# Two score products for the second attention: by query for the maxima, turned for the exponentials

## What is computed

```python
q = (query @ w_q.T).reshape(B, T_q, 16, 32)
k = (kv_source @ w_k.T).reshape(B, T_kv, 16, 32)
v = (kv_source @ w_v.T).reshape(B, T_kv, 16, 32)
attn = softmax(einsum('bqhd,bkhd->bhqk', q, k) * 32 ** -0.5, axis=-1)
out = einsum('bhqk,bkhd->bqhd', attn, v).reshape(B, T_q, 512)
return out @ w_o.T
```

## Time and profile before

| | us |
|---|---|
| timed runs, median of 3 | 1249.32 (1249.26 to 1250.52) |
| profiled execution, span | 1257.6 |
| of it, attention1 by itself, t=4 to t=29 | 276.1 to 558.2 |
| PE busy over the span | 1189.3 (95%) |
| DVE, ACT, POOL busy | 950.4 (76%), 708.7 (56%), 589.7 (47%) |

### The profile page before, as it was taken

How to read it: one execution, slowest core, us unless ns; L and a number is a source line. 1 busy time by engine, 2 the same in 40 slices (tenths; PEclk the granted TensorE clock), 3 DMA queues, 4 the chain that set the end, 5 groups by cost and what they waited for, 6 DMA issues and landing times.

```text
span 1257.6 us, 29419 instructions
## 1 busy us (share of the span) xinstructions
PE 1189.3 (95%) x10692; PEld 822.8 (65%) x10692; DVE 950.4 (76%) x2006; ACT 708.7 (56%) x1988; POOL 589.7 (47%) x685
## 2 busy tenths in 40 slices
PE   6888998799999999999999999999999998799996
PEld 3555665588888888786444445777777776466663
DVE  5889898899999999896677777777777775445460
ACT  4377788799899999896344322222222231365552
POOL 0047668737666667733200000445544345466744
PEclk9999999999999999999999999999999999899999
DMA  9522033134445454643870141221314320799987
GB/s 346 210 60 76 1 32 46 43 111 142 165 135 169 159 172 148 181 157 119 153 196 1 41 127 34 68 44 60 69 34 108 96 68 2 220 254 242 256 139 96
DMA packets 157567, 150.28 MB, mean 119 GB/s; under 512 B 78544, under 2 KB 111472, under 8 KB 157424
## 3 DMA queue, kind: packets, MB, share of 16 engines
q1 hardware_dynamic: 139584, 125.94, 35.5%
q0 software_dynamic: 13248, 21.15, 8.9%
q10 hardware_dynamic: 4592, 1.32, 0.6%
HBM read 84.93 MB, written 57.19 MB: 113 GB/s over the span
## 4 chain that ended last, share of the span: by engine, by line
PE 59%; DMA 17%; issue 8%; DVE 8%; POOL 5%; ACT 3%; ACTq 0%; SPq 0%; POOLq 0%; DVEq 0%
PE bank L121 28%; DMA lists<-att_land 14%; PE bank L1503 6%; PE bank L2125 5%; PE bank L955 4%; POOL lists L1629 4%; PE bank L1435 4%; PE bank L1456 3%; PE bank L1450 2%; PE bank L1421 2%; DMA q_rows<-att_land 1%; PE bank L1024 1%; ACT att_land L1353 1%; PE bank L872 1%; PE bank L891 1%
## 5 line engine op out<-in xcount | busy, mean ns | idle before, releaser
L1629 POOL DMA_INDIRECT lists<-att_land x128 | 134.4, 1050 | 310.7 <-DVE att_land L1770 166.8
L1353 ACT ACTIVATE att_land<-bank,att_land 128x120 f32<-128x120 f32 x512 | 178.3, 375 | 11.3 <-DVE att_land L1221 11.2
L2125 PE MATMUL bank<-att_land 128*128 128x512 f16 x768 | 177.3, 381 | 0.6 <-DVE program_logits L1304 0.6
L1952 ACT ACTIVATE att_land<-program_x 128x512 f32<-128x512 f32 x40 | 25.2, 631 | 195.2 <-DVE program_x L2094 165.1
L2125 PEld LDWEIGHTS bank<-att_land 128*128 128x128 f16 x768 | 75.4, 98 | 82.9 <-issue 2.0
L121 PE MATMUL bank<-program_xs,program_wgu 128*128 128x512 f16 x576 | 128.7, 379 | 0.6 <-DVE att_land L1729 0.6
L1353 ACT ACTIVATION_READ_ACCUMULATOR att_land<-bank,att_land 128x1 f32 x512 | 112.8, 221 | 0.0
L121 PE MATMUL bank<-att_land 128*128 128x128 f16 (+1 forms) x1560 | 101.0, 221 | 0.5 <-DVE att_land L1278 0.5
L121 PEld LDWEIGHTS bank<-program_xs,program_wgu 128*128 128x128 f16 x576 | 56.2, 98 | 67.5 <-DVE att_land L1729 1.1
L1221 DVE TENSOR_REDUCE att_land<-bank 128x4 f32<-128x480 f32 x128 | 82.4, 644 | 20.5 <-PE bank L1421 20.1
L1503 PE MATMUL bank<-att_land 128*128 128x512 f16 x384 | 93.4, 379 | 0.0
(11 more groups left out here) (305 smaller groups left out, 2817.2 us busy)
## 6 DMA issues: line engine op xcount, KB each, us to landing
att_land<-q_rows SPq DMA_DIRECT2D x96, 128.0 KB, 2.6
xn_rows<-att_land SPq DMA_DIRECT2D x37, 256.0 KB, 3.7
out_rows<-att_land SPq DMA_DIRECT2D x37, 256.0 KB, 6.4
q_rows<-att_land SPq DMA_DIRECT2D x32, 256.0 KB, 2.9
xt_tiles<-att_land SPq DMA_DIRECT2D x32, 256.0 KB, 2.1
x_rows<-program_x SPq DMA_DIRECT2D x8, 1024.0 KB, 4.8
att_land<-x_rows SPq DMA_DIRECT2D x8, 1024.0 KB, 5.6
program_xs<-xt_tiles SPq DMA_DIRECT2D x28, 256.0 KB
```

The lines of the kernel that those rows point to most:

```text
L1353: last = act.activation(prob[:, c, h, :], ps_s[c % 2][:, h, :], ACT.Exp, bias=nmax[:, u % 2, c, h:h + 1], accum_out=rsum[:, u % 2, n:n + 1])
L1629: pool.indirect_dma_start(out=io["lists"], out_offset=bass.IndirectOffsetOnAxis(ap=index[:, t, k:k + 1], axis=0), in_=load[:, t, k, :], in ...
L2125: last = pe.matmul(ps_y[i][:, :], hid[:, c % 2, a, i * P:(i + 1) * P], wd[:, q, c, :], start=c == 0 and n == 0, stop=c == NC - 1 and n == 2)
```

## The change

`scores` stays, but its result only gives maxima. VectorE splits the negated maxima, divided by 64, into a high and a low f16 part and turns them in blocks of 32x32 (`maxima_turned`); SyncE copies them with four DMAs into partitions 96 and 97 of the packed queries. The keys have the constant 64 in these two rows. `scores_turned` multiplies keys (stationary, 98 rows, 120 columns) by queries (128 columns), so that scores less their maxima come out with the context rows on the partitions; ScalarE takes the exponential twice from PSUM (`exponentials`), once as float32 and once as f16. The transposes and the per-head exponentials with sums go. Residues of groups 0 to 2 are made by GpSimd, of group 3 by VectorE, both from SBUF. The values get a 33rd column of ones, which gives the row sums; head 0 has its own place in another bank (`first_output`). Both norms are applied by ScalarE in one operation (`normalise`), after a tiny one on GpSimd. The weight conversion's three operations go into three steps. There are three packed query buffers, the third in space of `program_xs`; so the second batch of tokens in `shared` waits for all outputs. The orders of all five streams within a step change; JOIN and TAIL don't. Some semaphores of `front` are used again.

```diff
+def key_constants(pool, g, n):
+    two = struct.unpack("<f", struct.pack("<ee", MS, MS))[0]
+    return pool.memset(g.keys[:, n].rearrange("p r n -> p (r n)").bitcast(f32), two)
...
-    spread(sp, g.queries[:, u % 2], io["q_rows"][u], (0, 0, 1), done[u % 2])
+    spread(sp, g.queries[u % 3], io["q_rows"][u], (0, 0, 1), done[u % 3])
...
+        if u < self.first:
+            return
+        pool.wait_ge(self.root, u + 1)
+        pool.tensor_scalar(self.shift[:, d], self.mv[:, d, 0:1], self.rstd[:, d], -1.0, ALU.mult,
+                           ALU.mult).then_inc(self.shifted, 1)
+    def normalise(self, act, g, u):
+        act.wait_ge(self.shifted, u + 1 - self.first)
+        act.activation(self.xn[:, u % 2], g.x[:, u, :], ACT.Identity, scale=self.rstd[:, u % 4],
+                       bias=self.shift[:, u % 4]).then_inc(self.ok, 1)
...
+    prob = g.early(7 * D, [P, SLOTS, HC, P])
+    nmax = g.early(7 * D + SLOTS * D, [P, 2, HC, KC])
+    parts = g.early(7 * D + SLOTS * D + 2 * HEADS, [P, 2, 2 * HEADS], f16)
+    turned = g.early(7 * D + SLOTS * D + 4 * HEADS, [P, 2, 2 * HEADS], f16)
...
+    ps_rest = ps_o[:, DH // 2 + 1:D].rearrange("p (h n) -> p h n", h=HEADS - 1)
+    ps_sum = ps_o[:, DH // 2:D:DH + 1]
...
                 sp.wait_ge(q_out[u % 2], 16 * (u // 2 + 1))
-                need(sp, c4["s_mm"], KC * (u - 1))
...
                 packed_queries(sp, g, io, u, q_in)
+            if live(t):
+                sp.wait_ge(s["m_tr"], t + 1)
+                to = g.queries[t % 3][96:98].rearrange("p r (c n) -> p (r c) n", c=KC)
+                for n in range(KC):
+                    rows = slice(32 * n, 32 * n + 32)
+                    sp.dma_start(to[:, :, rows], turned[rows, t % 2, :]).then_inc(m_in[t % 2], 16)
             if live(v):
...
+        def prob_low(u, c):
+            if live(u):
+                n = KC * u + c
+                pool.wait_ge(c4["p_hi"], n + 1)
+                pool.wait_ge(c4["exp"], n + 1)
+                pool.tensor_tensor(pT[0:J, c, 1], prob[0:J, n % SLOTS], pT[0:J, c, 0], ALU.subtract).then_inc(c4["p_lo"], 1)
...
-                need(pool, rows_out[u % 2], 16 * (u // 2))
-                need(pool, s["g_tr"], u - 1)
-                apply(lg, s["mean_g"], u)
+            if t == 1:
+                pool.wait_ge(f.a["exp"], NT)
+                pool.wait_ge(f.q["y_ok"], NT)
+                key_constants(pool, g, 1).then_inc(f.key_ones, 1)
+            u = t + 4
+            if live(u):
+                ln.inverse_root(pool, g, u, u % 4)
...
-            if live(u):
-                ln.inverse_root(pool, g, u, u % 4)
-            u = t + 3
-            if live(u) and u >= HEAD:
-                if u == HEAD:
-                    pool.wait_ge(ln.ok, HEAD)
-                need(pool, s["xt_mm"], u - 1)
...
+            if 4 < t <= 3 * B + 2 and t % 3 == 2:
+                b = t // 3 - 1
+                need(pool, w_hi, b + 1)
+                pool.tensor_tensor(g.wgu[:, b, 1, :], raw[:, :], g.wgu[:, b, 0, :], ALU.subtract).then_inc(w_lo.handle, 1)
+            prob_low(t - 1, 1)
+            if 0 < t <= 3 * B and t % 3 == 0:
+                b = t // 3 - 1
+                need(pool, w_in, 16 * (b + 1))
+                pool.tensor_tensor(raw[:, :], raw[:, :], g.ws[:, :].to_broadcast([P, IS]), ALU.mult).then_inc(w_scaled.handle, 1)
+            prob_low(t - 1, 2)
...
...
+            dve.wait_ge(c4["max"], KC * u + KC)
+            row = nmax[:, u % 2].rearrange("p r c -> p (r c)")
+            high, low = (parts[:, u % 2, n * HEADS:(n + 1) * HEADS] for n in range(2))
+            dve.tensor_scalar(high, row, 1 / MS, None, ALU.mult).then_inc(s["m_part"], 1)
+            dve.wait_ge(s["m_part"], 2 * u + 1)
+            dve.scalar_tensor_tensor(low, row, 1 / MS, high, ALU.mult, ALU.subtract).then_inc(s["m_part"], 1)
+            dve.wait_ge(s["m_part"], 2 * u + 2)
+            need(dve, m_in[u % 2], TURN * (u // 2))
+            dve.transpose(turned[:, u % 2, :], parts[:, u % 2, :]).then_inc(s["m_tr"], 1)
...
+        def prob_low(u, c):
+            if live(u):
+                n = KC * u + c
+                dve.wait_ge(c4["p_hi"], n + 1)
+                dve.wait_ge(c4["exp"], n + 1)
+                dve.tensor_tensor(pT[0:J, c, 1], prob[0:J, n % SLOTS], pT[0:J, c, 0], ALU.subtract).then_inc(c4["p_lo3"], 1)
...
+                need(dve, s["of"], 2 * (u - 1))
+                dve.reciprocal(rinv[:, u % 2, :], ps_sum).then_inc(s["inv"], 1)
...
-                dve.tensor_tensor(of[:, :].rearrange("p (h o) -> p h o", h=HEADS),
-                                  ps_o[:, :].rearrange("p (h o) -> p h o", h=HEADS),
-                                  rinv[:, u % 2, :].rearrange("p (h o) -> p h o", o=1).to_broadcast([P, HEADS, DH]),
...
         def step(t):
-            maximum(t - 1, 3)
-            prob_low(t - 1, 0)
+            maximum(t, 0)
             query_low(t + 1)
+            maximum(t, 1)
             rows_low(t + 2)
             yield
-            prob_low(t - 1, 1)
-            maximum(t, 0)
             weighted(t - 2)
+            maximum(t, 2)
             logits(t - 5)
-            maximum(t, 1)
-            prob_low(t - 1, 2)
-            residual(t - 3)
-            gate_stats(t - 3)
-            maximum(t, 2)
             aggregate(ln, t + 5)
             stats(ln, t + 6)
             first_rows(t + 3)
-            prob_low(t - 1, 3)
+            maximum(t, 3)
+            maxima_turned(t)
+            residual(t - 3)
+            gate_stats(t - 3)
             output_low(t - 2)
...
...
+        def exponentials(u, c):
             if not live(u):
                 return
-            act.wait_ge(c4["p_mm"], KC * u + c + 1)
-            need(act, c4["o_mm"], KC * (u - 1) + PLACE[c] + 1)
+            n = KC * u + c
+            act.wait_ge(c4["t_mm"], n + 1)
+            before = n - SLOTS
+            if before >= 0:
+                low_done(act, before // KC, before % KC)
+            act.activation(prob[0:J, n % SLOTS], ps_p[c % 2][0:J], ACT.Exp).then_inc(c4["exp"], 1)
+            need(act, c4["o_mm"], (KC + 1) * (u - 1) + (c + 1 if c else KC + 1))
...
         def step(t):
-            prob_high(t - 1, 0)
             query_high(t + 1)
             rows_high(t + 2)
+            exponentials(t - 1, 0)
             yield
-            prob_high(t - 1, 1)
-            exps(t - 1, 3)
-            prob_high(t - 1, 2)
-            exps(t, 0)
-            exps(t, 1)
-            prob_high(t - 1, 3)
+            exponentials(t - 1, 1)
+            gate_normalised(t - 4)
+            exponentials(t - 1, 2)
+            rows_normalised(t + 3)
             output_high(t - 2)
+            exponentials(t - 1, 3)
             gate_high(t - 4)
-            exps(t, 2)
...
+        def scores_turned(u, c):
...
-            need(pe, c4["p_lo"], KC * u + c - 1)
+            if c == 0:
+                pe.wait_ge(m_in[u % 2], TURN * (u // 2 + 1))
+                if u % TB == 0 and b < 2:
+                    pe.wait_ge(f.key_ones, b + 1)
+            need(pe, c4["exp"], KC * u + c - 1)
+            need(pe, c4["p_hi"], KC * u + c - 1)
             for h in range(HC):
-                last = pe.transpose(ps_p[c % 2][0:J, h, :], prob[:, c, h, :], g.ident[:, :])
-            last.then_inc(c4["p_mm"], 1)
+                last = pe.matmul(ps_p[c % 2][0:J, h, :], g.keys[0:3 * DH + 2, b % 2, h, c * J:(c + 1) * J],
+                                 g.queries[u % SLOTS][0:3 * DH + 2, h, c * P:(c + 1) * P], start=True, stop=True)
+            last.then_inc(c4["t_mm"], 1)
...
+            low_done(pe, u, c)
+            b = u // TB
             for h in range(HC):
-                cols = slice((c * HC + h) * DH, (c * HC + h + 1) * DH)
-                for n, (a, b) in enumerate(((0, 0), (0, 1), (1, 0))):
-                    last = pe.matmul(ps_o[:, cols], pT[0:J, c, a, h, :], g.v1[0:J, b, u // TB, cols],
-                                     start=n == 0, stop=n == 2)
+                head = c * HC + h
+                high, low = g.v1[0:J, b, head, :], g.v1_low[b][0:J, head * DH:(head + 1) * DH]
+                if head == 0:
+                    continue
+                at = (DH + 1) * head - DH // 2
+                pe.matmul(ps_o[:, at:at + DH + 1], pT[0:J, c, 0, h, :], high[:, 0:DH + 1], start=True, stop=False)
+                pe.matmul(ps_o[:, at:at + DH], pT[0:J, c, 0, h, :], low, start=False, stop=False)
+                last = pe.matmul(ps_o[:, at:at + DH + 1], pT[0:J, c, 1, h, :], high[:, 0:DH + 1], start=False, stop=True)
             last.then_inc(c4["o_mm"], 1)
+        def first_output(u):
...
+            for n in range(2):
+                pe.matmul(ps_o[:, DH // 2:DH // 2 + 1], pT[0:J, 0, n, 0, :], high[:, DH:DH + 1], start=n == 0, stop=n == 1)
+            pe.matmul(ps_first(u), pT[0:J, 0, 0, 0, :], high[:, 0:DH], start=True, stop=False)
+            pe.matmul(ps_first(u), pT[0:J, 0, 0, 0, :], low, start=False, stop=False)
```

(29 more changed lines are left out.)

216 lines of the change are left out of this document (121 added, 95 removed).

## The result

The changed kernel takes 1296.72 us (median of 4 runs, 1295.41 to 1297.49), the kernel before 1249.78 (4 runs, 1249.26 to 1250.52): a ratio of 1.0357, 95% interval 1.0334 to 1.038. The forecast was 1244, the range 1226 to 1261, the chance of slower 0.34. It is 47 us slower and 53 above the forecast, outside the range and beyond every rival.

What follows compares the result with a forecast made beforehand. TensorE's own work was taken to bound the second attention; 26 steps of 9.93 us plus queue, conversion and token-load terms gave -2.8, with -1.6 and -1 at the ends -5.4 together: 1244 us, range 1226 to 1261.

Steps and rivals of the forecast that it cites:

- TensorE's step: Second attention, one 128-token tile: TensorE's own work falls from 10.71 to 9.93 us, -0.78 in each of 26 steps.
- Rival 3: New turned products: the slow 120-column weight load isn't hidden, 109 ns a product, step 10.76, 1254 us; chance 0.08.
- except for head 0, two more small matmuls: +0.05: Row sums on TensorE: free through a 33rd values column, only head 0 needs two small matmuls, +0.05 us a step.
- everything else: Semaphores, places of the values, and the second batch of tokens held until all outputs: costed at nothing.
- The hold-up of the low part: VectorE's two-SBUF-input operation excludes GpSimd, so the maxima wait some 0.9 us; 0.2 us in steps with conversions.
- rival 4: VectorE bounds the step by exclusion, two operations each waiting a whole GpSimd operation: step 10.6, 1251 us; chance 0.12.
- SyncE's queue: Packed queries needed 2.5 us sooner, late behind big transfers: 17.2 us of TensorE waits over the 26 steps.
- Rival 2: Maximum, split, turn, four DMAs and product form a one-step loop that sets the step, middle 11.0: 1259 us; chance 0.22.
- The join: First four tiles beside the front, where VectorE and ScalarE set the time and get lighter: -1 us, bounds -4 and +4.
- The token loads: Step t=26, where ScalarE issues the token loads: +1.0 us.
- GpSimd's residues: Residues between exponential and output product, costed at nothing; if GpSimd is 0.3 us late, 0.3 a step.
- Two last steps: Steps 31 and 32, their latency under the shared FFN's first matmuls: -1.6 us.

Runs made afterwards that it cites:

- Experiments 1: Changed kernel with VectorE making query_low ahead of maximum(t,0) instead of after it: 1291.55 us, ratio 1.0265 to the kernel before.
- 6: Changed kernel with head 0's output in free columns of the scores' first bank and head 0 scaled first: 1289.43 us, ratio 1.0205 to the kernel before.
- Experiments 5: Changed kernel with the gate's transposes behind the queries' second half on TensorE: 1295.65 us, ratio 1.0239 to the kernel before.
- experiment 4: Changed kernel with GpSimd's weight conversions behind both residues of the step: 1287.01 us, ratio 1.0234 to the kernel before.
- experiment 8: Changed kernel with the edits of experiment 4, Experiments 5 and 6 together: 1285.56 us, ratio 1.0163 to the kernel before.
- 10: On top of experiment 8: x_rows transfers cut to one tile a step, sh_guT issued behind q_rows: 1273.66 us, ratio 1.0097 to the kernel before.
- experiment 11: Edits of experiment 8, 9 and 10 together, and first_output one place later, behind scores_turned(t-1,0): 1269.17 us, ratio 1.0059 to the kernel before.
- 14: experiment 11 plus x_rows and keys' packing issued where SyncE waits, scores(t,2) behind queries(t+2,0), maximum(t,2) behind the norms: 1273.97 us, ratio 1.0126.
- Experiment 3: Changed kernel with the front's last residual ahead of two half steps of residues on GpSimd: 1295.11 us, ratio 1.027 to the kernel before.
- 9: On top of experiment 8: TensorE's first half of attention step 1 behind the front's remaining products, plus Experiment 3's edit: 1282.85 us, ratio 1.0168.

## Why the prediction was wrong

**TensorE's step** (9.93): right as work, 9.94 by the rows. Rival 3 (weight load) is out.

**Failed: "except for head 0, two more small matmuls: +0.05"**, and with it "everything else (... the places of the values ...) I cost at nothing". Head 0's place in the queries' bank is a handover of a bank between TensorE and VectorE in every step, 0.55 us, that the whole diff shows (a `need` on q_lo in `first_output`, one on `of` in `queries`) and that I priced as two matmuls. Experiments 1 and 6 show it: moving `query_low` moves the wait, another bank takes it away (10.95 to 10.50).

**Failed: the new order of the streams, which "everything else ... I cost at nothing" takes in.** Output transposes and a score group had been TensorE's work between `product` and the gate transposes, behind which the residual was hidden. They moved ahead, one group of transposes there shrank to turned products, and the gate transposes now wait 0.46 us, through the held-up split 1.02 and 1.29. Experiments 5 (10.47) and 4 (the two longer ones are gone) show it. The removed transposes themselves were priced rightly at 1.76. 0.78 saved, 0.55 + 0.77 (the mean of the 26) paid, and 0.44 for the rarer waits in the table and the clock: that is 10.71 to 11.69.

**VectorE.** The hold-up of the low part was foreseen at 0.9 and measured at 0.91 over its free 0.17 in 15 of 26 steps and at 1.58 in four; that of the high part, 0.94 in seven, wasn't foreseen, and I let both delay only the maxima, worth 0.2 us in steps with conversions, not the residual behind them. The signs that I gave for rival 4 came (TensorE waits for VectorE in every step, the low part takes over 1 us in most), but as put it is out: experiment 4 took 20 us from VectorE and the shortest step stayed. The signs don't tell a full engine from one whose order is wrong.

**SyncE's queue** (17.2 us): 3.1 in the changed kernel, since its steps were 1.8 us longer than 9.93, but 19.7 once they had shrunk (experiment 8), 3.6 with the large transfers moved (10). The term was real, but for a kernel that wasn't there. That 17.1 for q_rows in experiment 8 comes so near to 17.2 is partly luck: its steps were 10.2 at the shortest and 11.5 in the mean, not 9.93, and by my own sum should have waited less. **Rival 2** (the maxima's round trip sets the step, 1259): no wait of that kind in the 26 steps after; once at the join, 3.16 us. It comes up when the rest is mended (experiments 11 and 14: up to 6 us). Its issues cost 0.61 to 0.64 us each, beyond my bounds (0.35 to 0.6).

**The join** (-1, bounds ±4): +8.1, twice the bound. I looked at the load of VectorE and ScalarE and not at the order: a wait of 3.2 us, the residual behind it, 4.2 for `weighted`, and a lower clock after both. Experiment 3 alone gives back next to nothing, 9 2.7 us, 11 nearly all (49.9 against 47.1).

**The token loads** (+1.0 at t=26): four issues keep ScalarE's queue for 3.39 us, `query_high` stands behind them, and step 27 takes 14.37 us, 3.4 over the shortest; before, it took 12.79 against 10.71. **GpSimd's residues**, put at nothing, cost 2.5 us in two steps.

**Two last steps** (-1.6): step 30 alone is +2.6, by waits of the same kinds.

**The sum** has a slip: 258.2 + 17.2 + 2.6 + 1.0 is 279.0, not 279.4. It changes nothing here.

What stays open: whether 9.93 can be reached. Single steps of 10.03 occur, no kernel's mean is under 11.0. In experiment 11 the 26 steps take 28.6 us more than 26 times 9.94, of which TensorE's waits name 17.7. Each wait removed by order brought up another: the banks first, then SyncE's order of packing and small DMAs. Giving those issues to another queue wasn't tried. Nor is it settled what makes the part from t=31 to the end longer: the forecast carried the change of the attention over one to one, and no experiment tests that.

## What to carry to other kernels

When a change takes work out of an in-order engine, list for each instruction behind it which semaphore it needs and how much of the removed or moved work had covered that need; and when it puts a result into a bank that others use, follow the bank, not the instruction, round the step: writer, reader, next writer. A sum of busy times finds neither. Price the waits of a queue for the step you expect and also for the one you would get if it is longer: slack appears and disappears with it.
